# A second norm that moves from ScalarE to VectorE, with bias passes of full height and GpSimd's products behind the statistics: eight linear-attention layers on one core

## The reference

```python
q = phi(h @ wq + bq); k = phi(h @ wk + bk); v = h @ wv + bv        # 16 heads of 8
kv = einsum('bshd,bshm->bhdm', k, v)
z = 1.0 / (einsum('bshd,bhd->bsh', q, k.sum(axis=1)) + 1e-06)
h = ln(h + einsum('bshd,bhdm,bsh->bshm', q, kv, z) @ wo + bo)      # first norm
h = ln(h + gelu(h @ w1 + c1) @ w2 + c2)                            # second norm, F = 512
```

## Time and profile before

| | us |
|---|---|
| median of three runs | 1039.72 |
| the profiled execution | 1038.53 |
| its span, first to last instruction | 1036.6 |
| PE busy (5782 matmuls) | 950.8 |
| ScalarE busy | 777.6 |
| VectorE busy | 750.1 |
| GpSimd busy | 301.4 |

### The profile page before, as it was taken

The page is one execution under the profiler, slowest core; times in us unless marked ns, Lnnn a source line. Parts: engine busy times, 40 slices in busy tenths (PEclk is TensorE's granted clock), DMA queues, the critical chain, the costliest instruction groups (busy, mean ns, idle before and its releaser), DMA issues.

```text
span 1036.6 us, 18947 instructions
## 1 busy us (share of the span) xinstructions
PE 950.8 (92%) x5782; PEld 755.7 (73%) x5782; DVE 750.1 (72%) x2466; ACT 777.6 (75%) x1333; POOL 301.4 (29%) x299
## 2 busy tenths in 40 slices
PE   3569999999899998999899998999899999999980
PEld 2447887778777887778777886788777887787650
DVE  6867777777677767677677767677677778778646
ACT  2457888888788887888788887888788888888622
POOL 5103222322233222232233222232223222345513
PEclk9879999999999999999999999999999999999965
DMA  4100100000000100001000100001000000000002
GB/s 143 54 9 15 36 1 1 19 6 32 1 18 0 36 1 0 18 0 35 1 18 0 36 1 0 18 0 35 1 17 1 0 0 2 1 1 2 1 0 81
DMA packets 22440, 16.67 MB, mean 16 GB/s; under 512 B 3964, under 2 KB 18280, under 8 KB 22376
## 3 DMA queue, kind: packets, MB, share of 16 engines
q1 hardware_dynamic: 22376, 16.00, 5.2%
HBM read 13.89 MB, written 2.10 MB: 15 GB/s over the span
## 4 chain that ended last, share of the span: by engine, by line
PE 66%; ACT 13%; DVE 12%; issue 7%; DVEq 0%; DMA 0%; POOL 0%; POOLq 0%; ACTq 0%
PE down_ps L639 17%; PE q_ps L598 6%; PE q_ps L580 5%; PE k_ps L574 5%; ACT z_tm L767 4%; ACT L794 4%; PE att_ps L610 3%; PE up_ps L627 3%; PE up_ps L629 3%; PE up_ps L628 3%; PE small_ps L587 3%; DVE st L821 3%; PE t_ps L617 3%; PE small_ps L592 3%; PE down_ps L635 3%
## 5 line engine op out<-in xcount | busy, mean ns | idle before, releaser
L639 PEld LDWEIGHTS down_ps<-w_use,hid 128*128 128x128 f32 x2048 | 243.2, 192 | 44.9 <-issue 44.9
L639 PE MATMUL down_ps<-w_use,hid 128*128 128x128 f32 x2048 | 255.8, 278 | 0.0
L709 ACT ACTIVATE hid<-up_ps 128x512 f32<-128x512 f32 x256 | 144.8, 589 | 70.7 <-PE up_ps L629 64.5
L860 POOL TENSOR_TENSOR res_ffn<-z_tm,g_ffn 128x512 f32<-128x512 f32 x64 | 104.7, 1635 | 302.9 <-DVE z_tm L842 302.9
L853 POOL TENSOR_TENSOR res_att<-z_tm,g_att 128x512 f32<-128x512 f32 x64 | 82.4, 1288 | 351.4 <-DVE h L809 351.3
L816 DVE TENSOR_TENSOR h<-down_ps,res_ffn 128x512 f32<-128x512 f32 x64 | 44.2, 691 | 112.7 <-ACT z_tm L767 112.7
L821 DVE BATCH_NORM_STATS2 st<-h 128x6 f32<-128x128 f32 x512 | 110.9, 279 | 2.2
L627 PE MATMUL up_ps<-z_hi,w_hi 128*128 128x512 f32 x256 | 111.9, 437 | 0.4 <-DVE gate_bc L488 0.3
L767 ACT ACTIVATE z_tm<-h,shift,rstd 128x128 f32<-128x128 f32 x256 | 105.6, 483 | 2.9 <-DVE shift L834 2.1
L629 PE MATMUL up_ps<-z_lo,w_hi 128*128 128x512 f32 x256 | 101.6, 397 | 0.0
L628 PE MATMUL up_ps<-z_hi,w_lo 128*128 128x512 f32 x256 | 100.5, 393 | 0.0
(11 more groups left out here) (170 smaller groups left out, 1755.4 us busy)
## 6 DMA issues: line engine op xcount, KB each, us to landing
raw_w<-in_L_attn_W SPq DMA_DIRECT2D x16, 256.0 KB, 4.7
x_tm<-in_L_attn_x SPq DMA_DIRECT2D x4, 512.0 KB, 5.9
bias_bc<-in_L_attn_c SPq DMA_DIRECT2D x8, 256.0 KB, 4.3
out_y<-gate_tm SPq DMA_DIRECT2D x8, 256.0 KB, 2.0
raw_g<-in_L_attn_g SPq DMA_DIRECT2D x15, 64.0 KB
raw_att<-in_L_attn_Wq SPq DMA_DIRECT2D x8, 64.0 KB, 1.8
raw_att<-in_L_attn_Wk SPq DMA_DIRECT2D x8, 64.0 KB, 1.8
raw_att<-in_L_attn_Wv SPq DMA_DIRECT2D x8, 64.0 KB, 1.9
```

Of the source, the lines that this page charges most:

```text
L639: last = nc.tensor.matmul(down_ps[:, t, :], hid[:, j, t * P:(t + 1) * P], w2_use[:, j, :], start=False, stop=(j == FC - 1 and t == TT - 1))
L709: nc.scalar.activation(hid[:, j, :], up_ps[j % 2][:, :], ACT.Gelu).then_inc(s["gelu"], 1)
L860: nc.gpsimd.tensor_tensor(res_ffn[:, b % 2, :, :], z1_tm[:, :, :], g_ffn[:, :].unsqueeze(1).to_broadcast([P, TT, D]), ALU.mult).then_inc(s ...
```

## The change

- `act_norm2` is gone. `dve_norm2` does the second norm on VectorE, after `dve_z1_lo` and ahead of `dve_q_phi` and `dve_h2` (the sums).
- VectorE's order: both sets of statistics, then both aggregations, then `dve_g_copy`; `dve_split_w1` goes ahead of `dve_blocks`; `dve_k_phi` goes ahead of `dve_kvo` and `dve_q_n`.
- `pe_up` makes its four chunks in one call; the third goes to the bank of `k_ps`. `pe_k` comes right behind `pe_kz`, and `pe_down` is cut in 1, 1 and 2 chunks.
- The bias passes are functions of their own (`pe_down_bias`, `pe_att_bias`) and come between `pe_up` and `pe_kz`, with the waits that belong to them. `ones_r`, `row_att` and `row_ffn` are 128 partitions high; rows 2 to 127 of the bias rows are zeros, which GpSimd writes once at the start (three more instructions there, and CONSTS is 16).
- `pool_res_att` waits for `mv1_s`, the aggregates of the first norm, in place of `h1_s`. `pool_res_ffn` is for unit p - 2 in place of p - 1, behind `pool_w2` and behind `pool_res_att`, and has one buffer.
- At the end, the experts' second product uses `t_ps` in place of `k_ps`.

```diff
@@ -93,8 +93,10 @@
         w2_use = sb("w2_use", [P, FC, D])
         g_att = sb("g_att", [P, D])
         g_ffn = sb("g_ffn", [P, D])
-        row_att = sb("row_att", [2, TT, D], F32R)
-        row_ffn = sb("row_ffn", [2, TT, D], F32R)
+
+        row_att = sb("row_att", [P, TT, D], F32R)
+        row_ffn = sb("row_ffn", [P, TT, D], F32R)
+        zeros = sb("zeros", [P, D])
         fin_bc = sb("fin_bc", [P, 4, D])
@@ -570,6 +574,8 @@
             pe.wait_ge(s["zfm"], u + 1)
             if after_first(u):
                 pe.wait_ge(s["kphi"], u)
+            if is_unit(u - 3):
+                pe.wait_ge(s["gelu"], (u - 3) * FC + 3)
             for t in range(TT):
                 last = nc.tensor.matmul(k_ps[:, t, :], z_fm[:, b % 2, t * P:(t + 1) * P], w_qk[:, D:2 * D], start=True, stop=True)
             last.then_inc(s["kproj"], 1)
@@ -600,10 +606,17 @@
         def pe_kvo(pe, u):
             nc.tensor.matmul(KVO_PS, blk[:, 0, :], w_o[:, :], start=True, stop=True).then_inc(s["kvo_ps_s"], 1)
 
-        def pe_att(pe, u):
+        def pe_att_bias(pe, u):
             if after_first(u):
                 pe.wait_ge(s["h1_s"], u)
             nc.tensor.matmul(att_flat, ones_r[:, :], row_att[:, :, :].rearrange("p t d -> p (t d)"), start=True, stop=False)
+
+        def pe_down_bias(pe, u):
+            if after_first(u):
+                pe.wait_ge(s["h2_s"], u)
+            nc.tensor.matmul(down_flat, ones_r[:, :], row_ffn[:, :, :].rearrange("p t d -> p (t d)"), start=True, stop=False)
+
+        def pe_att(pe, u):
             pe.wait_ge(s["kvo_sb"], u + 1)
             pe.wait_ge(s["qn"], u + 1)
             for t in range(TT):
@@ -617,22 +630,24 @@
                 last = nc.tensor.transpose(t_ps[:, t * P:(t + 1) * P], z1_tm[:, t, :], ident[:, :])
             last.then_inc(s["t1_ps"], 1)
 
-        def pe_up(pe, u, chunks):
-            if chunks[0] == 0:
-                pe.wait_ge(s["z1lo_s"], u + 1)
-            for j in chunks:
-                if after_first(u) or j >= 2:
-                    pe.wait_ge(s["gelu"], u * FC + j - 1)
+
+        up_bank = (up_ps[0][:, :], up_ps[1][:, :], k_ps[:, :, :].rearrange("p t d -> p (t d)"), up_ps[0][:, :])
+
+        def pe_up(pe, u, keys):
+            pe.wait_ge(s["z1lo_s"], u + 1)
+            if after_first(u):
+                pe.wait_ge(s["gelu"], u * FC)
+            for j in range(FC):
+                if j == 2:
+                    pe.wait_ge(s["kphi"], keys)
+                if j == 3:
+                    pe.wait_ge(s["gelu"], u * FC + 1)
                 w_hi, w_lo = w1_hi[:, j * P:(j + 1) * P], w1_lo[:, j * P:(j + 1) * P]
-                nc.tensor.matmul(up_ps[j % 2][:, :], w_hi, z1_hi[:, :], start=True, stop=False)
-                nc.tensor.matmul(up_ps[j % 2][:, :], w_lo, z1_hi[:, :], start=False, stop=False)
-                nc.tensor.matmul(up_ps[j % 2][:, :], w_hi, z1_lo[:, :], start=False, stop=True).then_inc(s["up"], 1)
+                nc.tensor.matmul(up_bank[j], w_hi, z1_hi[:, :], start=True, stop=False)
+                nc.tensor.matmul(up_bank[j], w_lo, z1_hi[:, :], start=False, stop=False)
+                nc.tensor.matmul(up_bank[j], w_hi, z1_lo[:, :], start=False, stop=True).then_inc(s["up"], 1)
 
         def pe_down(pe, u, chunks):
-            if chunks[0] == 0:
-                if after_first(u):
-                    pe.wait_ge(s["h2_s"], u)
-                nc.tensor.matmul(down_flat, ones_r[:, :], row_ffn[:, :, :].rearrange("p t d -> p (t d)"), start=True, stop=False)
             for j in chunks:
                 pe.wait_ge(s["gelu"], u * FC + j + 1)
                 for t in range(TT):
@@ -650,11 +665,19 @@
             if ffn:
                 if b == 2:
                     pe.wait_ge(s["w1_split"], l * 2 + 2)
-                pe_up(pe, p - 2, (0, 1))
+                pe_up(pe, p - 2, p + 1 if att else UNITS)
+                if b == 2:
+                    pe.wait_ge(s["w2_ready"], l * 2 + 2)
+                pe_down_bias(pe, p - 2)
             if att:
+                if b == 0:
+                    pe.wait_ge(s["ratt_ready"], l + 1)
+                pe_att_bias(pe, p)
                 pe_kz(pe, p, b)
-            if ffn:
-                pe_up(pe, p - 2, (2, 3))
+            if proj:
+                if b == SEQS - 1:
+                    pe.wait_ge(s["qk_ready"], l + 2)
+                pe_k(pe, p + 1, b + 1)
             if b == 4 and is_layer(l + 1):
                 pe.wait_ge(s["zfm"], p + 2)
                 pe_fold_att(pe, l + 1)
@@ -665,19 +688,15 @@
                 if b == 0:
                     pe.wait_ge(s["vo_ready"], l * 2 + 2)
                 pe_kv_ksum(pe, p)
-            if proj:
-                if b == SEQS - 1:
-                    pe.wait_ge(s["qk_ready"], l + 2)
-                pe_k(pe, p + 1, b + 1)
+            if ffn:
+                pe_down(pe, p - 2, (0,))
             if att:
                 pe_den(pe, p)
                 pe_kvo(pe, p)
             if between:
                 between()
             if ffn:
-                if b == 2:
-                    pe.wait_ge(s["w2_ready"], l * 2 + 2)
-                pe_down(pe, p - 2, (0, 1))
+                pe_down(pe, p - 2, (1,))
             if ln1:
                 if b == 4 and is_layer(l + 1):
                     pe.wait_ge(s["fold_a"], l + 2)
@@ -689,8 +708,6 @@
             if ffn:
                 pe_down(pe, p - 2, (2, 3))
             if att:
-                if b == 0:
-                    pe.wait_ge(s["ratt_ready"], l + 1)
                 pe_att(pe, p)
             if state:
                 if isinstance(p, int) and p <= 0:
@@ -794,8 +804,6 @@
                 nc.scalar.preload_act_table_set("gelu_and_others")
             if between:
                 between()
-            if ln2:
-                act_norm2(act, p, p - 3, (b - 3) % SEQS)
             if state:
                 act_state_copy(act, p + 2, (b + 2) % SEQS)
@@ -813,12 +821,14 @@
             dve.wait_ge(s["t1m"], u + 1)
             if after_first(u):
                 dve.wait_ge(s["z2n"], TT * u)
-            nc.vector.tensor_tensor(h2[:, :, :], down_ps[:, :, :], res_ffn[:, b % 2, :, :], ALU.add).then_inc(s["h2_s"], 1)
-
-        def dve_norm_stats(dve, h, first, ready, count, st_s, mv_s, done):
+            nc.vector.tensor_tensor(h2[:, :, :], down_ps[:, :, :], res_ffn[:, :, :], ALU.add).then_inc(s["h2_s"], 1)
+
+        def dve_stats_of(dve, h, first, ready, count, st_s):
             dve.wait_ge(ready, count)
             for t in range(TT):
                 nc.vector.bn_stats(st[:, first + t, :], h[:, t, :]).then_inc(s[st_s], 1)
+
+        def dve_aggr_of(dve, first, st_s, mv_s, done):
             dve.wait_ge(s[st_s], TT * done + TT)
             dve.sem_inc(s["dve_waited"], 1)
             for t in range(TT):
@@ -842,6 +852,13 @@
                 nc.vector.tensor_scalar(z1_tm[:, t, :], h1[:, t, :], rstd[:, t:t + 1], shift[:, t:t + 1],
                                         ALU.mult, ALU.add).then_inc(s["z1n"], 1)
 
+        def dve_norm2(dve, p, b):
+            dve.wait_ge(s["shift_s"], p)
+            for t in range(TT):
+                i = TT + t
+                nc.vector.tensor_scalar(z_tm[:, b, t, :], h2[:, t, :], rstd[:, i:i + 1], shift[:, i:i + 1],
+                                        ALU.mult, ALU.add).then_inc(s["z2n"], 1)
+
         def dve_z1_lo(dve, u):
             dve.wait_ge(s["z1hi_s"], u + 1)
             nc.vector.tensor_tensor(z1_lo[:, :], t_ps[:, :], z1_hi[:, :].bitcast(F32), ALU.subtract).then_inc(s["z1lo_s"], 1)
@@ -849,15 +866,15 @@
         def pool_res_att(pool, u, b):
             z_ready(pool, u)
             if after_first(u):
-                pool.wait_ge(s["h1_s"], u)
+                pool.wait_ge(s["mv1_s"], TT * u)
             nc.gpsimd.tensor_tensor(res_att[:, :, :], z_tm[:, b, :, :], g_att[:, :].unsqueeze(1).to_broadcast([P, TT, D]),
                                     ALU.mult).then_inc(s["t2m"], 1)
 
         def pool_res_ffn(pool, u, b):
-            if after_first(u) and after_first(u - 1):
-                pool.wait_ge(s["h2_s"], u - 1)
+            if after_first(u):
+                pool.wait_ge(s["h2_s"], u)
             pool.wait_ge(s["z1n"], TT * (u + 1))
-            nc.gpsimd.tensor_tensor(res_ffn[:, b % 2, :, :], z1_tm[:, :, :], g_ffn[:, :].unsqueeze(1).to_broadcast([P, TT, D]),
+            nc.gpsimd.tensor_tensor(res_ffn[:, :, :], z1_tm[:, :, :], g_ffn[:, :].unsqueeze(1).to_broadcast([P, TT, D]),
                                     ALU.mult).then_inc(s["t1m"], 1)
 
         def pool_period(pool, l, b):
@@ -869,13 +886,13 @@
                 pool_res_att(pool, p, b)
             if b == 0 and is_unit(p) and in_use:
                 pool_row_att(pool, l, True)
+            if b == 2 and is_unit(p) and in_use:
+                pool_w2(pool, l, True)
+            if is_unit(p - 2):
+                pool_res_ffn(pool, p - 2, (b - 2) % SEQS)
             if b == 1 and is_layer(l) and in_use:
```

(73 more changed lines are left out.)

2 lines of the change are left out of this document (1 added, 1 removed).

## The result

The changed kernel takes 1114.62 us (median of four runs, 1113.47 to 1116.54), the kernel before beside it 1041.49. The ratio is 1.07, with a 95% interval of 1.0653 to 1.0747. The forecast of 1104 is 10.6 us short, inside its range. The fourth execution of the kernel before took 1046.07 us, above the range given at the start.

A forecast was written before the change was run, and what follows sets the result against it. PE and the h2-to-`g_sb` handshake were taken as nearly level, DVE's loop setting the new period. Terms -36 + 29 + 36 + 8 + 10 + 17 = +64 on 1038.5 gave 1102.5, 1104 us as median; range 1067 to 1128.

The forecast's parts named there:

- The two waits: PE's bias passes wait for GpSimd's rows: +4.18 us at b = 0, +5.10 at b = 2, seven times each: +29 and +36.
- The clock: Longer PE idle at the 14 waits brings 10 more falls of the granted clock: +17 us, bounds 0 and +20.
- my sum of the three terms: The waits at b = 0 (+29 us) and b = 2 (+36) and the clock (+17).
- The regular period: DVE's loop, closing through `dve_k_phi`, sets 13.5 us in place of 14.11; over 60 periods -36 us.
- its four parts: Loop steps: k_e to h1 5.22 us, h1 to `pe_kv_ksum` 3.19, PE 2.49, ScalarE 2.62.
- the rival of 1018: PE sets the regular period at its 12.73 us and the waits shrink: 1018 us; chance 0.06.
- `k_e`: On DVE, taken as 0.43 us long where its row shows 1.34, because GpSimd's overlapping `res_ffn` now runs earlier.
- the rival of 1158: k_e still collides with GpSimd's product, 0.9 us a period: 1158 us; chance 0.03.
- b = 3 to 5: Affines between h2 and h1 (0.71 us) and two folds, formerly hidden, enter the loop: 1.2 a layer, +8 us.
- The last four attention periods: Final norm's statistics and norm join DVE's loop, plus a GpSimd collision of 0.9: +10 us, bounds +6 and +16.

The follow-up runs named there:

- rows_first: The changed kernel with GpSimd's attention row (b = 0) and down weights and row (b = 2) written ahead of the residual product: 1031.51 us, ratio 0.9907.
- qn_first: rows_first with the split of W1 behind the blocks and kvo and q_n ahead of k_phi on VectorE: 975.07 us, ratio 0.9372.
- low_bias: The changed kernel with both bias passes contracting over 2 rows again, at their new place: 1140.88 us, ratio 1.0967.
- before_full: The kernel before with the bias passes at full height and nothing else: 1016.26 us, ratio 0.9748.
- res_att_h1: The changed kernel with GpSimd's attention product behind h1 again in place of behind the aggregates: 1076.85 us, ratio 1.0313.
- split_behind: The changed kernel with the split of W1 (b = 1) behind the blocks again: 1109.28 us, ratio 1.0644.
- norm2_act: rows_first with the second norm on ScalarE again, behind the gelu table's load: 1039.84 us, ratio 0.9963.
- before_two: The kernel before with bias passes at full height in their old places and the second norm on VectorE: 994.6 us, ratio 0.9541.

## Why the prediction was right

- *The two waits* were the cause. I had 4.18 and 5.10 us more per layer; PE's bias passes start 4.3 and 5.7 us later than in rows_first, 70 us where I had 29 + 36 = 65.
- *The clock.* I had ten more falls for 17 us; there were twelve more, one at each of the 14 waits where two of the loop edges had one before. The 14 cost 21.6 us if all behind the bias passes is the clock's. Waits and clock together are 92 us; rows_first gives 7 of them back at b = 1, and so is 83 faster (86 by the spans), where my sum of the three terms was 82.
- *The regular period*: 13.53 against 13.5, set by the loop through `k_phi` (qn_first), with the bias passes at 0.23 (low_bias, before_full). The term was right, though three of its four parts were off by 0.07 to 0.15 and cancel. PE does not set the regular period, and the rival of 1018 falls.
- *`k_e`* came out at 0.465 us in the mean, 1.3 before. The rival of 1158 falls.
- *b = 3 to 5*: by the starts of h1 they take 14.26, 13.68 and 14.4, 1.75 a layer above 13.53. The kernel before has 14.82, 14.11 and 14.38, which is 0.98 above its 14.11. So the change adds 0.8 a layer, and 0.2 more at b = 6, where I had 1.2.
- *Missed: b = 1.* The change puts `dve_split_w1` ahead of `dve_blocks`, and I gave it no term. It costs 1.74 x 7 = 12 us (res_att_h1 and split_behind take it away). I had used the collision with GpSimd to explain `k_e`, and did not ask what else the products, moved by 3 us, would now lie over. This one term is as large as the whole error.
- *The last four attention periods*: the first three are 17.57, not 16.5, the fourth 16.41. The final norm takes 3.21 beside GpSimd where I had allowed 1.04 + 0.9. Their +13.9 stands against +10.
- *Two gains that I had at nothing.* Behind the last h2 the kernel is 9.0 us shorter, mostly by the clock. And an edge of the hardware loop costs 3.1 us over a regular period in the kernel before, 2.0 in rows_first: 6 us at five edges.
- *How near the number is* owes something to luck: 12 at b = 1, 5 each at the waits and the clock and 4 at the end are too low in my sum, and these two gains stand against them.
- *Sizes that my later expectations missed*: for norm2_act I had a regular period of 13.9 to 14.1 and it is 13.75; for before_two I had 12.8, level with PE's work, and it is 13.0.

## What to carry to other kernels

When one engine stops being the bound, add up the loop that closes from period to period, step by step; what a change saves on any engine ends there. When a wait is moved earlier in an in-order queue, look not at the regular period but for the operand that is written once in a while, and at what stands ahead of its writer: a product that nobody needed yet cost 83 us because a bias row stood behind it. When a GpSimd instruction is moved, list what VectorE runs in its new place; even the order that mended the waits laid one over the second norm. And before a difference of some microseconds is given to an edit, compare the granted clock of the parts that the edit did not touch.

## What was not expected of the hardware

- A matmul whose weights are 2 rows high costs 0.20 us more, and so does the next group of full height (0.42 and 1.09 against 0.23 and 0.89). Two low ones in a row share it: 0.42, 0.24, then 1.09.
- These VectorE instructions, which go from SBUF to SBUF, take two to three times as long beside a GpSimd product: cast 0.42 to 1.27, subtraction 0.69 to 1.64, four 128x128 norms 1.11 to 3.21. ScalarE's final norm beside one took 1.65, as its second norm did in the kernel before.
- Around idle stretches of PE of 3.7 to 6.0 us, the granted clock fell to 1.2 GHz 14 times in 14; at the loop edges in the trace of before_full (an execution of 1023.73 us), 3.1 to 3.3 us, five times in five; at those of the kernel before, 2.7 to 2.9 us, twice in five. A fall lasted 3.4 or 6.8 us; one of 3.4 us at b = 2 cost 0.7 to 1.0 us, one of 6.8 us 2.3.
- Behind the last h2, the same 56 matmuls kept PE busy 10.2 us with the clock at 1.2 GHz for 24 us of the stretch, and 19.4 with it there for 45; the stretch took 36.6 and 45.5.
